# A Mamba block between two RWKV FFNs: in eight of 64 steps GpSimd does the product by C

## The chip, the cores and the metric

The kernel runs on one core of one Trainium2 chip. The metric is the device time of a run in microseconds. TensorE is called PE here, VectorE DVE, ScalarE ACT, GpSimd POOL and SyncE SP, as in the profile.

## What is computed

An input of 4 sequences of 2048 tokens with 512 features goes through an FFN, a selective state space layer (16 states for each of 1024 inner channels), and the same FFN again. All is float32. Cut to what matters:

```python
def _L0_attn_ref(x, ln_w, ln_b, W_in, W_conv, b_conv, W_xproj, W_dt, b_dt, A_log, D_skip, W_out):
    xn = _layernorm(x, ln_w, ln_b)
    xs, z = jnp.split(jnp.einsum('bld,ed->ble', xn, W_in), 2, axis=-1)
    xp = jnp.pad(xs, ((0, 0), (K_CONV - 1, 0), (0, 0)))
    xc = silu(b_conv + sum(xp[:, k:k + L, :] * W_conv[:, k] for k in range(K_CONV)))   # 4 taps
    dbl = jnp.einsum('ble,re->blr', xc, W_xproj)                                       # x projection
    dt_low, B_ssm, C_ssm = dbl[..., :32], dbl[..., 32:48], dbl[..., 48:]
    delta = softplus(jnp.einsum('blr,er->ble', dt_low, W_dt) + b_dt)
    dA = jnp.exp(delta[..., None] * -jnp.exp(A_log))
    dBx = delta[..., None] * B_ssm[:, :, None, :] * xc[..., None]
    # for each t: h = dA_t * h + dBx_t;  y_t = einsum('bdn,bn->bd', h, C_t)
    y = (ys + D_skip * xc) * silu(z)
    return jnp.einsum('ble,de->bld', y, W_out) + x

def _ffn(x):   # x_prev is x one token earlier
    xr, xk = mu_r * x + (1 - mu_r) * x_prev, mu_k * x + (1 - mu_k) * x_prev
    return sigmoid(xr @ W_r.T) * (square(relu(xk @ W_k.T)) @ W_v.T)

x = x + 0.5 * _ffn(_layernorm(x))
x = x + _L0_attn_ref(_layernorm(x), ...)
x = x + 0.5 * _ffn(_layernorm(x))
```

## The kernel before

**Tiling.** The tokens are cut into 16 chunks of W = 512 tokens. The program is a pipeline over iterations: in iteration `it` the scan of chunk `it` runs, beside it the front of chunk `it + 1` (`f`: first FFN, xs, convolution, x projection) and the back of chunk `it - 1` (`b`: output projection, second FFN). The iterations before chunk 0 and behind chunk 15 hold what is left of these. An iteration has 64 steps: step `s` is state `s % 16` of a quarter `s // 16` of the 1024 channels, 256 channels as two tiles of 128 partitions, so that an operation of the scan is 128 x 1024.

**A step.** POOL makes `dbx` = u times B (`product`, L1283; 4 buffers), ACT makes `decay` = exp(delta A) in PSUM (`make_decay`, L877; 2 buffers, three activations), DVE scans in place in `decay` (`scan`, L1078) and multiplies it by C into `g` (`weigh`, L1088; 2 buffers in SBUF), PE adds `g` into `y_acc` by eight transposes (`sum_g`, L556), and ACT keeps the last state (`save`, L892). ACT may make decay `s` once it has saved `s - 2`; POOL's product `s` waits for DVE's product by C of `s - 4`, and DVE's `weigh` of `s` for PE's sum of `s - 2`. B and C rows come from DRAM, a DMA from SP for each.

**Order.** Every engine executes its queue in order. What stands where is written in tables, one number or tuple for a kind of work: the step behind whose scan work it is put. `XS`, `TAP0`/`TAPS`, `ADD_HEAD`, `CTANH` and `CSILU` are the eight tiles of the convolution: PE's matmuls `xs`, ACT's `conv_start` (L792), DVE's three taps (L1031), POOL's `add_head` (L1262) and ACT's `conv_tanh` (L806) and DVE's `conv_silu` (L1034). POOL's `add_head(e)` stands in step `ADD_HEAD[e]`, one to four steps behind the taps, because POOL's queue runs some steps ahead of DVE's. `XPROJ` are the two halves of the x projection (`xproj`, L523), and `XROWS` = 51 is ACT's `x_rows` (L813), which takes it from PSUM. `keep_y` (L860) takes `y_acc` out in steps 17, 33, 49 and 65. `MM_K`, `MM_R`, `MM_V` are the FFNs' matmuls, `MIX_K`, `MIX_R` DVE's mixing before them, `TANH` and `RELU` ACT's. `MEANS` and `RSTD` end and use the statistics of a layer norm (POOL's Newton steps, some 18 small operations). Two PSUM banks, `mm`, go round among all matmuls by the table `BANK`: a group of matmuls waits until the work before it in its bank has been taken out. `ZEROS` says in which steps PE multiplies by a tile of zeros into `y_acc`: one such `add_zeros` is 128x512, two instructions in the profile, and doesn't change the sum.

## Time and profile before

| | us |
|---|---|
| median of 3 runs (lowest, highest) | 4895.8 (4893.4, 4898.2) |
| the profiled execution, device time | 4895.2 |
| its span from the first to the last instruction | 4893.2 |
| DVE busy in the span | 4486.8 |
| PE busy | 4290.6 |
| POOL busy | 3196.2 |
| ACT busy | 2899.1 |

The profile is one execution. Busy time of an engine leaves out waits, register and semaphore instructions. A row of the timeline has the start in us from the span's start, the time taken, the engine, line and operation, out<-in, and in brackets how long the engine had been idle and who released it. On one engine a row often starts a little before the one ahead of it has ended.

### The profile page before, as it was taken

What the parts mean: (1) busy time and instruction counts of PE and PEld (TensorE: products, weight loads), DVE (VectorE), ACT (ScalarE), POOL (GpSimd) and SP (SyncE); (2) the same over time, 40 slices, a digit from 0 to 9 for tenths busy, and PEclk for the clock granted to TensorE, in tenths of its full rate; (3) what the DMA queues carried; (4) which work ended last, traced back from release to release, by engine and by line L of the source; (5) the groups of instructions that cost most, each with busy time, mean ns of one, the idle gap of its engine ahead of it and who ended that gap; (6) DMA issues with size and microseconds to landing.
All of it is one profiled execution on the core that took longest, in us unless ns stands there. A gap on an engine that the chain in (4) does not pass through costs nothing.

```text
span 4893.2 us, 58099 instructions
## 1 busy us (share of the span) xinstructions
PE 4290.6 (88%) x16896; PEld 2377.8 (49%) x16896; DVE 4486.8 (92%) x3650; ACT 2899.1 (59%) x6355; POOL 3196.2 (65%) x3328
## 2 busy tenths in 40 slices
PE   6777999898999989989898899989989898999787
PEld 2444545454554545545454454545545454554443
DVE  2799999999999999999999999999999999999992
ACT  2555656566666666656666665666656666665452
POOL 1566767676675767767576776767767576776770
PEclk8888999999999999999999999999999999999798
DMA  2345555554554545555555554555555555555551
GB/s 82 128 142 181 171 164 184 172 182 163 188 170 154 189 157 188 175 171 188 161 177 161 188 171 151 190 176 179 173 180 178 153 180 159 188 170 152 166 164 62
DMA packets 423053, 810.71 MB, mean 166 GB/s; under 512 B 41264, under 2 KB 41264, under 8 KB 418640
## 3 DMA queue, kind: packets, MB, share of 16 engines
q1 hardware_dynamic: 422736, 807.00, 51.7%
q8 instruction: 136, 2.23, 0.2%
q14 instruction: 181, 1.48, 0.1%
HBM read 772.25 MB, written 34.60 MB: 165 GB/s over the span
## 4 chain that ended last, share of the span: by engine, by line
DVE 39%; PE 29%; issue 16%; ACT 7%; POOL 6%; DMA 2%; DVEq 0%; SPq 0%; POOLq 0%; ACTq 0%
DVE decay L1085 19%; DVE g L1093 10%; PE y_acc L567 6%; PE mm L494 5%; PE mm L483 5%; PE mm L472 4%; POOL dbx L1292 4%; DVE xc L1031 3%; PE mm L531 2%; DMA c_all<-bc_scratch 2%; PE mm L509 2%; PE mm L519 2%; DVE xc L1037 1%; ACT decay L889 1%; POOL xout L1281 1%
## 5 line engine op out<-in xcount | busy, mean ns | idle before, releaser
L1292 POOL TENSOR_TENSOR dbx<-u,b_all 128x1024 f32<-128x1024 f32 x1024 | 2414.2, 2358 | 902.4 <-DVE g L1093 901.6
L1085 DVE TENSOR_TENSOR_SCAN decay<-decay,state,dbx 128x1024 f32<-128x1024 f32 x1024 | 2404.4, 2348 | 179.5 <-ACT decay L889 178.0
L567 PE MATMUL y_acc<-ident,g 128*128 128x128 f32 x8192 | 1121.0, 282 | 380.2 <-DVE g L1093 378.4
L567 PEld LDWEIGHTS y_acc<-ident,g 128*128 128x128 f32 x8192 | 944.0, 144 | 946.8 <-DVE g L1093 721.9
L1093 DVE TENSOR_TENSOR g<-decay,c_all 128x1024 f32<-128x1024 f32 x1024 | 1243.1, 1214 | 9.1 <-issue 0.8
L886 ACT ACTIVATE decay<-delta,neg_a 128x512 f32<-128x512 f32 x1024 | 708.7, 692 | 36.8
L889 ACT ACTIVATE decay<-delta,neg_a 128x511 f32<-128x511 f32 x1024 | 686.9, 671 | 0.0
L895 ACT ACTIVATE state<-decay 128x2 f32<-128x2 f32 x1024 | 166.8, 163 | 511.2 <-DVE g L1093 509.0
L494 PE MATMUL mm<-wbuf_c,col 128*128 128x512 f32 x1024 | 461.0, 594 | 2.1 <-ACT col L758 1.3
L1031 DVE SCALAR_TENSOR_TENSOR xc<-mm,conv_sb,xc 128x509 f32<-128x509 f32 (+2 forms) x384 | 285.0, 742 | 46.6 <-ACT xs_last L804 35.3
L1296 POOL TENSOR_TENSOR dbx<-dbx,carry 128x1 f32<-128x1 f32 x1024 | 274.3, 268 | 80.3
L494 PEld LDWEIGHTS mm<-wbuf_c,col 128*128 128x128 f32 x1024 | 185.2, 190 | 191.9 <-issue 186.4
L802 ACT ACTIVATE xc<-mm,evec,conv_sb 128x512 f32<-128x512 f32 x128 | 99.4, 777 | 255.5 <-PE mm L509 221.3
L762 ACT ACTIVATE rows<-mm 128x512 f32<-128x512 f32 x128 | 76.2, 595 | 294.3 <-PE mm L483 294.3
L472 PE MATMUL mm<-mix_k,wbuf_c 128*128 128x512 f32 x512 | 233.2, 600 | 4.5 <-DVE mix_k L1008 4.4
L509 PE MATMUL mm<-xn_col,wbuf_d 128*128 128x512 f32 x512 | 235.2, 603 | 1.3 <-ACT xn_col L789 1.0
L483 PE MATMUL mm<-wbuf_d,xin 128*128 128x512 f32 x512 | 231.9, 597 | 4.4 <-DVE xin L1013 4.4
L596 PE MATMUL mm<-wbuf_a,gate 128*128 128x512 f32 x512 | 233.2, 599 | 2.2 <-issue 1.4
L472 PE MATMUL mm<-mix_k,wbuf_b 128*128 128x512 f32 x512 | 233.1, 599 | 1.7 <-DVE mix_k L1008 1.7
L509 PE MATMUL mm<-xn_col,wbuf_a 128*128 128x512 f32 x512 | 232.9, 599 | 1.4 <-DVE xc L1031 1.4
L519 PE MATMUL mm<-xn_col,wbuf_b 128*128 128x512 f32 x512 | 231.3, 595 | 0.0
L519 PE MATMUL mm<-xn_col,wbuf_c 128*128 128x512 f32 x512 | 230.7, 593 | 0.0
(100 smaller groups left out, 5098.7 us busy)
## 6 DMA issues: line engine op xcount, KB each, us to landing
b_all<-bc_scratch SPq DMA_DIRECT2D x1024, 256.0 KB, 3.4
c_all<-bc_scratch SPq DMA_DIRECT2D x1024, 256.0 KB, 3.6
wbuf_d<-in_w_r SPq DMA_DIRECT2D x32, 1024.0 KB, 7.2
wbuf_c<-in_w_v SPq DMA_DIRECT2D x32, 1024.0 KB, 7.2
xin<-in_x SPq DMA_DIRECT2D x16, 1024.0 KB, 7.0
wbuf_c<-in_w_k SPq DMA_DIRECT2D x16, 1024.0 KB, 6.6
wbuf_d<-in_w_in SPq DMA_DIRECT2D x16, 1024.0 KB, 5.7
wbuf_a<-in_w_in SPq DMA_DIRECT2D x16, 1024.0 KB, 8.1
```

The lines of the kernel that those rows point to most:

```text
L472: last = pe.matmul(bank(it, f"f{i}k{j}"), wk[:, ct, j * P:(j + 1) * P], mix_k[:, ct, :], start=ct == 0, stop=ct == CT - 1)
L483: last = pe.matmul(bank(it, f"f{i}r{tb}"), mix_r[:, ct, tb * P:(tb + 1) * P], wr[:, ct, :], start=ct == 0, stop=ct == CT - 1)
L494: last = pe.matmul(bank(it, f"f{i}v{tb}"), col[:, ct, tb * P:(tb + 1) * P], wv[:, ct, :], start=ct == 0, stop=ct == CT - 1)
L509: last = pe.matmul(bank(it, f"xs{e}"), win[:, ct, e % 4 * P:(e % 4 + 1) * P], xn_col[:, slot, ct, :], start=ct == 0, stop=ct == CT - 1)
L519: last = pe.matmul(bank(it, f"z{e}"), win[:, ct, e % 4 * P:(e % 4 + 1) * P], xn_col[:, slot, ct, :], start=ct == 0, stop=ct == CT - 1)
L567: last = pe.matmul(y_acc[:, tb, j * P:(j + 1) * P], g[:, s % PAIRS, j, tb * P:(tb + 1) * P], ident[:, :], start=n == 0 and j == 0 and tb % ...
L886: act.activation(d[:, 0, :], delta[:, q % 2, 0, :], ACT.Exp, scale=neg_a[:, e, n:n + 1]).then_inc(decay_done, 1)
L889: act.activation(d[:, 1, 1:W], delta[:, q % 2, 1, 1:W], ACT.Exp, scale=neg_a[:, e + 1, n:n + 1]).then_inc(decay_done, 1)
L1031: dve.scalar_tensor_tensor(out=o, in0=src[:, 0:W - late], scalar=conv_sb[:, e, q:q + 1], in1=o, op0=ALU.mult, op1=ALU.add).then_inc(m_dve. ...
L1085: dve.tensor_tensor_scan(d, d, flat(dbx[:, s % DBX, :, :]), state[:, batch, s, 0:1], ALU.mult, ALU.add).then_inc(scan_done, 1)
L1093: dve.tensor_tensor(g[:, s % PAIRS, :, :], decay[:, s % PAIRS, :, :], c_all[:, s % CRING, :].unsqueeze(1).broadcast_to([P, QT, W]), ALU.mu ...
L1292: pool.tensor_tensor(dbx[:, s % DBX, :, :], u[:, q % 2, :, :], b_all[:, s % BRING, :].unsqueeze(1).broadcast_to([P, QT, W]), ALU.mult).the ...
```

## The change

Eight steps of 64, 13, 29, 31, 35, 39, 41, 44 and 47 (`POOLED`), are treated in another way. All but 13 are steps with convolution taps on DVE. In these the scan writes its result to `g` in SBUF instead of in place in PSUM, so DVE's `scan` waits for PE's sum of `s - 2`, DVE has no `weigh`, and ACT no `save`. POOL, three steps later in its queue (behind its product `s + 3`), copies the last state (128x2) and multiplies `g` in place by C (`pool_weigh`). PE's sum, SP's load of C four steps on and POOL's product four steps on wait for whichever engine multiplies. ACT's decay of `s + 2` waits for the scan alone.

Beside that, entries of the tables move by a step or two, both halves of the x projection from 49, 50 to 47, 48, five zeros are added (20, 26, 37, 49, 52), and for chunk 1 the first layer norm moves: its POOL part to before `u`, its ACT part from step 58 of iteration -1 to behind the first step of iteration 0. The functions `ffn_norm`, `mamba_inner` and `make_res` are written for one tile at a time; where they stand is as before.

```diff
@@ tables @@
-        TURN = ((0, 0, 1, 1), (35, 35, 35, 35))
+        TURN = ((0, 0, 0, 1), (35, 35, 35, 35))
-        MM_R = ((10, 10, 12, 13), (41, 42, 44, 45))
+        MM_R = ((10, 11, 12, 13), (41, 42, 44, 45))
-        XPROJ = (49, 50)
-        ZEROS = {2: 2, 31: 2, 39: 2, 30: 1, 53: 1}
+        XPROJ = (47, 48)
+        ZEROS = {2: 2, 31: 2, 39: 2, 30: 1, 53: 1, 52: 1, 49: 1, 26: 1, 37: 1, 20: 1}
-        RELU = ((7, 8, 9, 10), (49, 50, 53, 53))
-        TANH = ((11, 13, 14, 14), (42, 43, 45, 46))
+        RELU = ((7, 8, 9, 10), (48, 50, 53, 53))
+        TANH = ((11, 14, 14, 14), (42, 43, 45, 46))
-        MIX_R = ((6, 7, 7, 8), (38, 39, 40, 40))
-        CSILU = (33, 34, 40, 42, 43, 45, 48, 48)
+        MIX_R = ((6, 7, 7, 8), (39, 40, 40, 40))
+        CSILU = (32, 34, 40, 42, 43, 45, 48, 48)
-        OUT_ADD = (6, 22, 23, 25)
-        STATS = ((51, 53, 53, 54), (9, 22, 24, 27), (18, 19, 20, 21))
+        OUT_ADD = (6, 21, 23, 25)
+        STATS = ((51, 53, 53, 54), (9, 22, 24, 27), (18, 18, 20, 21))
-        FFN_ADD = ((18, 19, 20, 22), (57, 58, 59, 60))
+        FFN_ADD = ((17, 19, 20, 22), (57, 58, 59, 60))
-        HISTORY = 26
+        HISTORY = 24
+        POOLED = (13, 29, 31, 35, 39, 41, 44, 47)
...
+        def so_far(it, s, pooled):
+            it, s = it + s // NSTEP, s % NSTEP
+            here = sum(q <= s for q in POOLED)
+            return it * len(POOLED) + here if pooled else it * (NSTEP - len(POOLED)) + s + 1 - here
...
+        def multiplied(it, s):
+            return (pool_mult_done if on_pool(s) else mult_done), so_far(it, s, on_pool(s))
...
@@ sum_g on PE (and likewise load_c on SP, product on POOL) @@
-                pe.wait_ge(mult_done, NSTEP * it + s + 1)
+                pe.wait_ge(*multiplied(it, s))
...
@@ make_decay and save on ACT @@
-                if due(count := NSTEP * it + s - PAIRS + 1):
+                if on_pool(s - PAIRS):
+                    if due(count := NSTEP * it + s - PAIRS + 1):
+                        act.wait_ge(scan_done, count)
+                elif due(count := so_far(it, s - PAIRS, False)):
                     act.wait_ge(saved, count)
...
             def save(it, s, batch):
+                if on_pool(s):
+                    return
...
@@ scan and weigh on DVE @@
-                dve.tensor_tensor_scan(d, d, flat(dbx[:, s % DBX, :, :]), state[:, batch, s, 0:1],
+                if on_pool(s) and due(count := NSTEP * it + s - PAIRS + 1):
+                    dve.wait_ge(g_summed, count)
+                o = flat(g[:, s % PAIRS, :, :]) if on_pool(s) else d
+                dve.tensor_tensor_scan(o, d, flat(dbx[:, s % DBX, :, :]), state[:, batch, s, 0:1],
                                        ALU.mult, ALU.add).then_inc(scan_done, 1)
             def weigh(it, s):
+                if on_pool(s):
+                    return
...
@@ POOL @@
+            def pool_weigh(it, s, batch):
+                pool.wait_ge(scan_done, NSTEP * it + s + 1)
+                pool.sem_inc(passed_pool, 1)
+                states = g[:, s % PAIRS, :, :]
+                pool.tensor_copy(state[:, batch, s, :], states[:, :, W - 1]).then_inc(pool_saved, 1)
+                pool.wait_ge(pool_saved, so_far(it, s, True))
+                pool.sem_inc(passed_pool, 1)
+                pool.wait_ge(c_loaded[s % CRING], it * (16 * NSTEP // CRING) + 16 * (s // CRING + 1))
+                pool.tensor_tensor(states, states, c_all[:, s % CRING, :].unsqueeze(1).broadcast_to([P, QT, W]),
+                                   ALU.mult).then_inc(pool_mult_done, 1)
...
                     if scn:
                         product(it, s)
+                        if s > 2 and on_pool(s - 3):
+                            pool_weigh(it, s - 3, bt)
...
                         if s == MAKE_U[0] + 64:
+                            if it == -1:
+                                ffn_rstd(0, 1)
                             make_u(f, 0, (bt + 1) % BATCHES)
-                    if ahead and s == RSTD[0]:
+                    if ahead and it != -1 and s == RSTD[0]:
                         ffn_rstd(0, it + 2)
...
@@ end of a step on ACT @@
-                    if ahead and s == NORM[0]:
-                        ffn_norm(0, it + 2)
+                    if ahead and it != -1:
+                        for n in at(NORM[0], s):
+                            ffn_norm(0, it + 2, n)
+                    if it == s == 0:
+                        for n in range(TB):
+                            ffn_norm(0, 1, n)
```

POOL, around step 32 of an iteration with scan, front and back, from the end of the second FFN's rstd (before L1216, after L1250) on. L1292 and L1296 (after: L1328 and L1332) are `product`, L1264 (after: L1298) is `add_head(0)`. First before, then after:

```order
L1216 TENSOR_SCALAR shift<-shift 128x4
L1292 TENSOR_TENSOR dbx<-u,b_all 128x1024
L1296 TENSOR_TENSOR dbx<-dbx,carry 128x1
L1292 TENSOR_TENSOR dbx<-u,b_all 128x1024
L1296 TENSOR_TENSOR dbx<-dbx,carry 128x1
L1264 TENSOR_TENSOR xc<-xc,head 128x3
L1292 TENSOR_TENSOR dbx<-u,b_all 128x1024
L1296 TENSOR_TENSOR dbx<-dbx,carry 128x1
```

```order
L1250 TENSOR_SCALAR shift<-shift 128x4
L1328 TENSOR_TENSOR dbx<-u,b_all 128x1024
L1332 TENSOR_TENSOR dbx<-dbx,carry 128x1
L1328 TENSOR_TENSOR dbx<-u,b_all 128x1024
L1332 TENSOR_TENSOR dbx<-dbx,carry 128x1
L1340 COPY state<-g 128x2
L1344 TENSOR_TENSOR g<-g,c_all 128x1024
L1298 TENSOR_TENSOR xc<-xc,head 128x3
L1328 TENSOR_TENSOR dbx<-u,b_all 128x1024
L1332 TENSOR_TENSOR dbx<-dbx,carry 128x1
```

The copy of the state and the product by C of step 29 stand between the product of step 32 and `add_head(0)`.

DVE, steps 28 to 31: L1085 (after: L1117) is `scan`, L1093 (L1127) `weigh`, L1042 (L1069) the gate's silu, L1031 (L1058) the taps. First before, then after:

```order
L1085 SCALAR_TENSOR_TENSOR decay<-decay,state,dbx 128x1024
L1042 SCALAR_TENSOR_TENSOR gate<-gate,mm 128x512
L1093 TENSOR_TENSOR g<-decay,c_all 128x1024
L1085 SCALAR_TENSOR_TENSOR decay<-decay,state,dbx 128x1024
L1031 SCALAR_TENSOR_TENSOR xc<-mm,conv_sb,xc 128x509
L1031 SCALAR_TENSOR_TENSOR xc<-mm,conv_sb,xc 128x510
L1031 SCALAR_TENSOR_TENSOR xc<-mm,conv_sb,xc 128x511
L1093 TENSOR_TENSOR g<-decay,c_all 128x1024
L1085 SCALAR_TENSOR_TENSOR decay<-decay,state,dbx 128x1024
L1042 SCALAR_TENSOR_TENSOR gate<-gate,mm 128x512
L1093 TENSOR_TENSOR g<-decay,c_all 128x1024
L1085 SCALAR_TENSOR_TENSOR decay<-decay,state,dbx 128x1024
```

```order
L1117 SCALAR_TENSOR_TENSOR decay<-decay,state,dbx 128x1024
L1069 SCALAR_TENSOR_TENSOR gate<-gate,mm 128x512
L1127 TENSOR_TENSOR g<-decay,c_all 128x1024
L1117 SCALAR_TENSOR_TENSOR g<-decay,state,dbx 128x1024
L1058 SCALAR_TENSOR_TENSOR xc<-mm,conv_sb,xc 128x509
L1058 SCALAR_TENSOR_TENSOR xc<-mm,conv_sb,xc 128x510
L1058 SCALAR_TENSOR_TENSOR xc<-mm,conv_sb,xc 128x511
L1117 SCALAR_TENSOR_TENSOR decay<-decay,state,dbx 128x1024
L1069 SCALAR_TENSOR_TENSOR gate<-gate,mm 128x512
L1127 TENSOR_TENSOR g<-decay,c_all 128x1024
L1117 SCALAR_TENSOR_TENSOR g<-decay,state,dbx 128x1024
```

The scan of steps 29 and 31 writes `g`, and no `weigh` follows the taps.

PE, steps 47 to 53: L567 (after: L583) is `sum_g`, L472 (L488) the matmuls k of the second FFN, L531 (L547) the halves of the x projection, L575 (L591) zeros, L543 (L559) dt. First before, then after:

```order
L472 MATMUL mm<-mix_k,wbuf_b 128x512 x4
L567 MATMUL y_acc<-ident,g 128x128 x16
L531 MATMUL mm<-xc,wx_sb 64x512 x4
L567 MATMUL y_acc<-ident,g 128x128 x8
L472 MATMUL mm<-mix_k,wbuf_b 128x512 x4
L531 MATMUL mm<-xc,wx_sb 64x512 x4
L567 MATMUL y_acc<-ident,g 128x128 x8
L472 MATMUL mm<-mix_k,wbuf_b 128x512 x4
L567 MATMUL y_acc<-ident,g 128x128 x16
L543 MATMUL mm<-xdbl,wdt_sb 128x512 x2
```

```order
L488 MATMUL mm<-mix_k,wbuf_b 128x512 x4
L547 MATMUL mm<-xc,wx_sb 64x512 x4
L583 MATMUL y_acc<-ident,g 128x128 x8
L547 MATMUL mm<-xc,wx_sb 64x512 x4
L583 MATMUL y_acc<-ident,g 128x128 x8
L591 MATMUL y_acc<-ident,zero 128x512
L583 MATMUL y_acc<-ident,g 128x128 x8
L488 MATMUL mm<-mix_k,wbuf_b 128x512 x4
L583 MATMUL y_acc<-ident,g 128x128 x8
L488 MATMUL mm<-mix_k,wbuf_b 128x512 x4
L583 MATMUL y_acc<-ident,g 128x128 x8
L591 MATMUL y_acc<-ident,zero 128x512
```

Before, the halves of the x projection stand on both sides of the third k; now both stand ahead of it, with a zero between, and another zero follows the fourth k.

## Rows read from the trace of the kernel before

**Rows 1.** The page, its first part: busy us, share of the span, instructions.

```profile
PE 4290.6 (88%) x16896; PEld 2377.8 (49%) x16896; DVE 4486.8 (92%) x3650; ACT 2899.1 (59%) x6355; POOL 3196.2 (65%) x3328
```

**Rows 2.** Costliest groups: count, busy us, mean ns of one, idle before, releaser.

```profile
L1292 POOL TENSOR_TENSOR dbx<-u,b_all 128x1024 f32<-128x1024 f32 x1024 | 2414.2, 2358 | 902.4 <-DVE g L1093 901.6
L1085 DVE TENSOR_TENSOR_SCAN decay<-decay,state,dbx 128x1024 f32<-128x1024 f32 x1024 | 2404.4, 2348 | 179.5 <-ACT decay L889 178.0
...
L1093 DVE TENSOR_TENSOR g<-decay,c_all 128x1024 f32<-128x1024 f32 x1024 | 1243.1, 1214 | 9.1 <-issue 0.8
```

**Rows 3.** Windows, chunks 0, 6, 15: length, busy us by engine, PEclk, DMA share, GB/s.

```profile
161.70:447.20 285.50, 214.39 (x860) 128.62 (x858) 268.01 (x202) 163.59 (x364) 193.53 (x191) 0.86 0.50 158
...
1905.40:2197.40 292.00, 264.08 (x1056) 145.94 (x1056) 280.05 (x229) 180.82 (x397) 199.72 (x207) 0.99 0.53 174
4531.50:4787.30 255.80, 201.16 (x844) 124.65 (x844) 243.59 (x168) 138.44 (x320) 172.70 (x148) 0.87 0.49 160
```

**Rows 4.** Windows of chunk 6, PE, PEld, DVE, ACT, POOL: steps 47-51, then 9-19.

```profile
2121.60:2147.10 25.50, 24.19 (x85) 11.39 (x85) 21.32 (x17) 12.96 (x31) 15.76 (x13) 1.00 0.73 240
...
1944.90:1992.10 47.20, 46.95 (x177) 25.53 (x176) 42.36 (x31) 27.89 (x63) 32.35 (x26) 1.00 0.52 163
```

**Rows 5.** Timeline, chunk 6, steps 13 to 15.

```profile
1963.36 3.67 PE L483 MATMUL mm<-wbuf_d,xn_col 128*128 128x512 f32 x8
...
1967.06 0.60 ACT L762 ACTIVATE rows<-mm 128x512 f32<-128x512 f32 x1 [3.85 <-PE mm L483]
...
1970.47 2.36 DVE L1085 TENSOR_TENSOR_SCAN decay<-decay,state,dbx 128x1024 f32<-128x1024 f32 x1 [3.62 <-ACT decay L889]
```

**Rows 6.** Timeline, chunk 6, steps 29 to 32.

```profile
2031.34 2.32 DVE L1031 SCALAR_TENSOR_TENSOR xc<-mm,conv_sb,xc 128x509 f32<-128x509 f32 x3
...
2031.74 2.37 POOL L1292 TENSOR_TENSOR dbx<-u,b_all 128x1024 f32<-128x1024 f32 x1
...
2034.32 0.20 POOL L1264 TENSOR_TENSOR xc<-xc,head 128x3 f32<-128x3 f32 x1
...
2034.55 0.63 ACT L811 ACTIVATE rows<-xc 128x512 f32<-128x512 f32 x1 [1.76 <-POOL xc L1264]
...
2039.21 1.02 PE L575 MATMUL y_acc<-ident,zero 128*128 128x512 f32 x2
...
2045.92 2.36 DVE L1085 TENSOR_TENSOR_SCAN decay<-decay,state,dbx 128x1024 f32<-128x1024 f32 x1 [0.30 <-ACT decay L889]
```

**Rows 7.** Timeline, chunk 6, steps 46 to 53.

```profile
2121.84 3.60 PE L472 MATMUL mm<-mix_k,wbuf_b 128*128 128x512 f32 x8
...
2132.11 1.09 PE L567 MATMUL y_acc<-ident,g 128*128 128x128 f32 x8 [1.31 <-DVE g L1093]
...
2144.85 0.69 ACT L820 ACTIVATE xdbl<-mm,xscale 64x512 f32<-64x512 f32 x1 [7.63 <-PE mm L531]
...
2147.11 2.36 DVE L1085 TENSOR_TENSOR_SCAN decay<-decay,state,dbx 128x1024 f32<-128x1024 f32 x1 [4.05 <-ACT decay L889]
...
2150.78 1.09 PE L567 MATMUL y_acc<-ident,g 128*128 128x128 f32 x8 [0.56 <-DVE g L1093]
```

**Rows 8.** Timeline of DVE and POOL, chunk 0, step 7; last row chunk 6, step 40.

```profile
190.05 2.34 DVE L1085 TENSOR_TENSOR_SCAN decay<-decay,state,dbx 128x1024 f32<-128x1024 f32 x1
192.31 2.76 DVE L1013 SCALAR_TENSOR_TENSOR xn_col<-col,vec,xn_col 128x512 f32<-128x512 f32 x2
...
191.52 2.34 POOL L1292 TENSOR_TENSOR dbx<-u,b_all 128x1024 f32<-128x1024 f32 x1
...
2087.77 1.57 DVE L1013 SCALAR_TENSOR_TENSOR xin<-col,vec,xin 128x512 f32<-128x512 f32 x2
```

**Rows 9.** Timeline of the start, POOL and DVE.

```profile
149.85 2.34 POOL L1270 TENSOR_TENSOR u<-delta,xc 128x1024 f32<-128x1024 f32 x1 [12.37 <-ACT delta L837]
...
161.74 2.36 DVE L1085 TENSOR_TENSOR_SCAN decay<-decay,state,dbx 128x1024 f32<-128x1024 f32 x1 [20.16 <-ACT decay L889]
```

99 lines of the change are left out of this document (54 added, 45 removed).

## The prediction

> **What bounds the kernel now.** I read the busy shares first [rows 1], then the costliest groups [rows 2], then the stretches of the program [rows 3, 4], and last the timeline at the places that the change touches [rows 5 to 9]. The reader is to see that DVE is busy for 92% of the span and PE for 88%, so neither has much to give. Of each step the scan costs 2.35 us and the product by C 1.21 us of DVE [rows 2]; a row begins 0.08 us before the one ahead of it ends (190.05 + 2.34 against 192.31 [rows 8]), so a product takes 1.13 us of the chain. Fourteen of the sixteen chunks are alike; the row of one of them, 292.0 us, stands for all [rows 3]: DVE busy 280.1, so idle 11.9; PE busy 264.1, so idle 27.9. Two of the DVE's waits make up most of its idle time. In step 15 it waits 3.62 us for a decay, which ACT makes only after a tanh whose matmul ends on PE at 1967.03 [rows 5]; PE is busy for 46.95 of 47.20 us there [rows 4]. In step 52 it waits 4.05 us for ACT, which had stood 7.63 us behind the x projection [rows 7].
>
> **What each part costs, if nothing else moves.** Eight products by C leave DVE: 8 x 1.13 = 9.0 us of a chunk. POOL takes on a copy of 128x2, by its other small operations 0.20 us [rows 6], and a product of 128x1024 with one operand broadcast, which is exactly the form of its product dbx<-u,b_all: 2.36 us [rows 2]; together about 2.65 us with the gaps of 0.08, so 21 us a chunk of an engine that is idle for 92 of 292 us. The x projection two steps sooner is to take away the 4.05 us. The five added zeros cost PE 0.87 to 0.93 us each (a zero is two instructions, 1.02 us [rows 6], less the overlap), 4.6 us a chunk. The scan that writes SBUF is not in the trace. Its bound comes from the DVE's other operations on PSUM and SBUF: the taps write SBUF, and their three take 2.32 us while POOL's product runs all the time beside them [rows 6]. I take 2.35 us, and 0.05 us either way for the range: 128 scans, 6 us. DMAs are not touched, except that a load of C is issued after POOL's product in a pooled step; it is four steps ahead of its use. The naive sum is (9.0 + 4.05) x 16 = 209 us. Most of it isn't to be had, for the reasons that follow.
>
> **Step 13: nothing.** The wait of step 15 hangs on PE's matmuls, which stand back to back from step 5 on. DVE arrives 1.13 us sooner and waits 4.75 instead of 3.62 us. POOL's product of step 13 begins after its product of step 16, near 1962.8, and ends near 1965.4, before PE has ended the matmul at 1967.03, behind which it asks for it [rows 5]. The zero of step 20 comes behind that stretch.
>
> **Steps 29 to 32: a loss of 2.8 us.** In POOL's queue the new product stands behind two products for dbx and ahead of add_head(0) [the order of POOL]. POOL is late here already: it had rstd work and works without a break until add_head(0) at 2034.32, and ACT waits 1.76 us for that before tanh(0), decay(31) and the gate [rows 6]. One DVE operation put into step 21 (an out_add, 0.6 us) delays the means, and all this queue, by another 0.6. So: dbx products of steps 31 and 32 end at 2034.9, copy and product for step 29 at 2037.55, add_head(0) at 2037.7, tanh(0) 2038.35, decay(31) 2039.7, gate tanh 2040.2. DVE, which stands at the gate in step 30, goes on 3 us later than it did. The tap of step 31 and ACT's four normalisations follow PE's xs; the scan of step 32 starts at 2048.7 instead of 2045.92 [rows 6]. Both pooled products before it have gained nothing.
>
> **Steps 33 to 47.** The same walk goes on with the durations of the trace. Step 35 gives 1.13 back, the zero in 37 and POOL's late product of 35 take it again (PE's transposes wait for it, then ACT, then the taps): scan 38 is 2.6 us late. In 38 to 41 DVE finds its old slack and two pooled steps: scan 42 is 0.5 us late. Then a collision counts. A DVE operation with two inputs in SBUF (mix_k, mix_r, silu) that starts while POOL's product runs ends only 0.55 us after it: two such take 1.57 us where POOL is about to end and 2.76 us where it has just begun [rows 8]. Before the change POOL starts its product right behind the DVE's, so it ends as the scan ends, and a collision costs 0.2 us. After a pooled step POOL goes straight on to its next dbx product, 5.7 us after the last product of DVE, and DVE's next two-input operation comes at 6.7 us. That happens in steps 42, 45 and 48, for some 1.1 us each: 3.3 us of the gain of the three. Scan 47 starts 1.3 us late and PE's first ffn_k matmul at 2123.3 instead of 2121.84 [rows 7].
>
> **Steps 48 to 63.** Now k1 and both halves of the x projection run on PE until 2139.1 (it was 2144.8), ACT isn't held by x_rows any more, and scan 52 comes at 2145.8 instead of 2147.11: the wait of 4.05 us is gone, but 1.2 us of the DVE's come back at keep_y of step 49, which waits for transposes that stand behind the first half of the projection. What is late next is PE. It was busy for 24.2 of the 25.5 us of steps 47 to 51 [rows 4] and had 1.31 + 0.56 us to spare until step 53 [rows 7]; the zeros of 49 and 52 take 1.8 us. So the matmuls of step 54 start 0.7 us later than they did, and from there to step 61 PE has no gap, and DVE follows it. The end of a chunk is then between 0 and 0.5 us late. I take 0 for each of the fourteen, with 2.2 us sooner (no collisions, POOL not late by the 0.6) and 2 us later as its bounds.
>
> **Start and ends.** In iteration -1 the rstd of chunk 1 now comes before u, when POOL waits 12.37 us anyway [rows 9], and ACT's four normalisations of that chunk come after the first decay. The first dbx product then starts at 152.4, right behind u, instead of behind the rstd, and the first scan at 155.1 instead of 161.74 [rows 9]: 6.6 us, once. Chunk 0 (285.5 us, DVE idle 17.5) and chunk 15 (255.8, idle 12.2) have only one of the FFNs beside the scan and PE at 75 to 79% [rows 3], so a part of their 9.0 us is real: I take 7 and 5 us, between 0 and 12 together as bounds below and 18 above.
>
> **Sum.** Against the profiled execution (4895.2 us, span 4893.2, median of the runs 4895.8): 14 x 0 + 6.6 + 7 + 5 = 18.6 us less, 4877 us.
>
> **A page of the notes.** The row of the collision is [rows 8]: 2.76 us for two operations that take 1.57 elsewhere. The Trainium skill, page "SBUF — State Buffer", section "Who interferes with whom", says that a VectorE instruction with two SBUF inputs and a GpSimd instruction that reads SBUF contend for one port pair, and that the second to issue fully blocks. By that rule, the trace agrees, the three collisions stand. If they cost only the usual 0.2 us, the chunk would end 2.2 us sooner, 4846 us. The same section says that an instruction with at most one SBUF input doesn't contend, which would leave the new scan alone; no row shows that scan.
>
> **Rivals.** (B) POOL isn't late where I have it late and the collisions stay small: each chunk ends 2.2 us sooner, 4877 - 31 = 4846 us; for it speaks POOL's idle third, against it [rows 6, 8]. (C) DVE was the bound all through, and the gains of 29 to 47 and the projection mostly arrive: 5.5 us a chunk, 4800 us; against it speaks PE's share in steps 47 to 61. (D) Slower: POOL's lateness is carried on. If its dbx product behind a pooled step is still late when the next one is due, the two-input operations of steps 34, 43 and 46 collide in full too, each for up to 1.2 us; 3.6 us less the slack of 1.6 is 2 us a chunk, 4877 + 28 = 4905 us. It decides once POOL is more than 0.9 us behind after the second product. (E) The change does nothing at all in the chunks but for the start: 4889 us; it lies within the forecast's own range.
>
> **How the numbers follow.** Forecast 0.45 (4865 to 4892), B 0.25, C 0.08, D 0.22. Within 0.2%, 9.8 us, a measurement of this kernel can hardly tell a difference. Faster than 4886: 0.34 of the forecast, B and C, 0.67; the same: 0.11 of the forecast and 0.07 of D, 0.18; slower 0.15. The range from 4825 to 4904 leaves out C and the far half of D, and holds the unknown of the scan.
>
> **What would show it.** In the changed profile: DVE's wait for ACT in step 52 gone; in step 30 a DVE wait of 3 us at the gate, and ACT's wait for add_head grown to 4 to 5 us; mix_k and silu in steps 42, 45 and 48 with 1.9 us in place of 0.9; DVE's wait in step 15 at 4.7 us; PE's gap of 0.56 us at step 52 gone; the first scan at 155 us. I am wrong if the scan into SBUF isn't 2.35 us, if POOL's product by C isn't 2.36 us, or if a typical chunk is not 290 to 294 us long.

## The result and the profile after

The changed kernel takes 4909.8 us (median of 10 runs, 4907.9 to 4913.1) against 4895.9 us (4892.2 to 4898.2) before: a ratio of 1.0029, 95% interval 1.0020 to 1.0037. It is slower by 0.3%, where 4877 us and a range up to 4904 had been predicted. The profiled execution spans 4907.1 us (4893.2 before).

The profile page of the changed kernel, its first part, against [rows 1]:

```profile
PE 4351.3 (89%) x17056; PEld 2423.2 (49%) x17056; DVE 4385.7 (89%) x3522; ACT 2882.0 (59%) x6227; POOL 3497.3 (71%) x3584
```

DVE has lost 101 us of work, POOL has gained 301, PE 61. The engine that was the busiest was relieved, and the kernel got longer. The costliest groups, against [rows 2]; L1344 is POOL's product by C, L1117 the scan in its two forms:

```profile
L1328 POOL TENSOR_TENSOR dbx<-u,b_all 128x1024 f32<-128x1024 f32 x1024 | 2414.8, 2358 | 746.2 <-DVE g L1127 738.2
L1117 DVE TENSOR_TENSOR_SCAN decay<-decay,state,dbx 128x1024 f32<-128x1024 f32 x896 | 2105.2, 2350 | 188.6 <-ACT decay L908 169.9
...
L1127 DVE TENSOR_TENSOR g<-decay,c_all 128x1024 f32<-128x1024 f32 x896 | 1089.0, 1215 | 15.9 <-PE y_acc L583 6.8
...
L1344 POOL TENSOR_TENSOR g<-g,c_all 128x1024 f32<-128x1024 f32 x128 | 301.6, 2356 | 24.0 <-POOL state L1340 22.9
L1117 DVE TENSOR_TENSOR_SCAN g<-decay,state,dbx 128x1024 f32<-128x1024 f32 x128 | 299.5, 2339 | 4.9 <-ACT decay L908 4.6
```

The windows of chunks 0, 6 and 15 (length; busy us of PE, PEld, DVE, ACT, POOL; granted clock, DMA share, GB/s), against [rows 3]:

```profile
153.00:434.20 281.20, 221.69 (x874) 133.24 (x874) 261.33 (x194) 163.54 (x359) 214.57 (x207) 0.86 0.51 164
1900.40:2193.60 293.20, 267.86 (x1066) 149.22 (x1066) 273.65 (x221) 179.86 (x389) 218.47 (x223) 0.99 0.53 173
4538.60:4799.10 260.50, 208.43 (x854) 127.60 (x854) 237.94 (x160) 136.79 (x312) 191.22 (x164) 0.87 0.48 157
```

DVE's idle time is 19.6 us in chunk 6 (11.9 before) and 22.6 in chunk 15 (12.2 before). The 13.9 us of the two spans divide as follows: the first scan comes 8.8 us sooner; chunk 0 is 4.2 us shorter; chunks 1 to 14 are 20.1 us longer together; chunk 15 is 4.7 us longer, and what follows its last scan 2.1 us.

To see where in a chunk that happens, I took the start of each scan from the timeline, counted from the chunk's first scan, as the mean of chunks 2 to 14, and subtracted the same of before:

| scan | 30 | 31 | 32 | 38 | 42 | 47 | 50 | 52 | 55 | 64 |
|---|---|---|---|---|---|---|---|---|---|---|
| changed, us late | -1.3 | 3.0 | 4.2 | 3.5 | 1.1 | 2.0 | 3.7 | -0.5 | 1.3 | 1.3 |
| predicted | | | 2.8 | 2.6 | 0.5 | 1.3 | | -1.3 | | 0 |

The first difference from the prediction arises by scan 32. First a row of the kernel before, whose xs of step 30 no row above shows, then the timeline of the changed kernel there, chunk 6 (start, us, engine and line; in brackets the idle time before and who ended it), against [rows 6]:

```profile
2035.77 3.60 PE L509 MATMUL mm<-xn_col,wbuf_d 128*128 128x512 f32 x8
```

```profile
2030.22 2.34 POOL L1344 TENSOR_TENSOR g<-g,c_all 128x1024 f32<-128x1024 f32 x1 [0.18 <-POOL state L1340]
2032.52 0.19 POOL L1298 TENSOR_TENSOR xc<-xc,head 128x3 f32<-128x3 f32 x1
...
2032.62 1.22 PE L583 MATMUL y_acc<-ident,g 128*128 128x128 f32 x8 [3.10 <-POOL g L1344]
2033.63 5.20 PE L525 MATMUL mm<-xn_col,wbuf_d 128*128 128x512 f32 x8
...
2032.74 0.63 ACT L827 ACTIVATE rows<-xc 128x512 f32<-128x512 f32 x1 [5.12 <-POOL xc L1298]
...
2038.87 0.78 ACT L818 ACTIVATE xc<-mm,evec,conv_sb 128x512 f32<-128x512 f32 x1 [3.70 <-PE mm L525]
...
2035.21 0.69 DVE L1069 SCALAR_TENSOR_TENSOR gate<-gate,mm 128x512 f32<-128x512 f32 x1 [4.46 <-ACT gate L891]
...
2045.40 2.36 DVE L1117 TENSOR_TENSOR_SCAN decay<-decay,state,dbx 128x1024 f32<-128x1024 f32 x1 [1.44 <-ACT decay L908]
```

Two chains start at POOL's product of step 29. One runs by add_head(0), which stands behind it on POOL, to ACT's tanh, decay(31) and the gate that DVE waits for. The other runs over PE, which has the sum of that g ahead of the eight matmuls of xs: it waits 3.10 us, and xs then takes 5.20 us where the same matmuls took 3.60 before. The windows of the wait, of the sum, and of xs (columns as above; the last three are clock, DMA share and GB/s):

```profile
2029.50:2032.60 3.10, 0.01 (x1) 0.00 (x0) 1.25 (x1) 0.00 (x0) 2.84 (x5) 1.00 0.55 172
2032.60:2033.80 1.20, 1.18 (x9) 1.19 (x10) 0.00 (x0) 1.05 (x2) 1.18 (x2) 0.85 0.14 51
2033.80:2038.80 5.00, 5.00 (x10) 2.07 (x9) 3.59 (x3) 1.37 (x4) 3.08 (x3) 0.69 0.36 124
```

After standing idle for 3.1 us, PE works for a while at the lower of its two levels, 1.2 GHz: a mean of 0.69 over the 5 us of xs. That differs from chunk to chunk: in chunks 2 to 14 xs of that step takes 3.6 to 5.3 us, 4.6 in the mean (3.6 in all of before). In chunks 3 and 9, where it takes 3.6, scan 32 is 2.8 and 2.9 us late; in the other eleven it is 4.2 to 4.8 us late. The Trainium skill, page "TensorE: Matmul & The Clock Gate", section "Part 1: The HAM clock gate", says that the array's clock goes back to half rate when the engine has been idle; the trace agrees here, with 0.69 behind the wait of 3.10 us.

The trace of the kernel before already had such places, at the start of a chunk, where I had not looked. In each of chunks 1 to 14 PE waits 2.55 to 2.88 us ahead of the sum in step 0, and in eight of the fourteen it then works at half clock: the transposes behind take up to 1.92 us, in the other six 1.04. Timeline and window of before, chunk 6, then the same place in chunk 5:

```profile
1905.56 1.33 PE L567 MATMUL y_acc<-ident,g 128*128 128x128 f32 x8 [2.55 <-DVE g L1093]
1906.69 1.92 PE L458 MATMUL mm<-ident,rows 128*128 128x128 f32 x8
...
1905.50:1909.90 4.40, 3.85 (x21) 3.45 (x22) 4.37 (x4) 4.28 (x10) 3.25 (x3) 0.61 1.02 276
...
1613.84 1.09 PE L567 MATMUL y_acc<-ident,g 128*128 128x128 f32 x8 [2.55 <-DVE g L1093]
1614.77 1.04 PE L458 MATMUL mm<-ident,rows 128*128 128x128 f32 x8
```

### The profile page after: what moved, and what is told of

The parts are those of the page before. It is cut to its first block, busy times and chain, and to the rows that moved or that the text cites. A ratio compares the mean times of both kernels' runs of the same rounds, so it can differ in the third digit from the quotient of the medians.

```text
span 4907.1 us, 58559 instructions
## 1 busy us (share of the span) xinstructions
PE 4351.3 (89%) x17056; PEld 2423.2 (49%) x17056; DVE 4385.7 (89%) x3522; ACT 2882.0 (59%) x6227; POOL 3497.3 (71%) x3584
## 4 chain that ended last, share of the span: by engine, by line
PE 38%; DVE 20%; POOL 17%; issue 14%; ACT 8%; DMA 3%; SPq 0%; DVEq 0%; POOLq 0%; ACTq 0%
POOL dbx L1328 10%; PE y_acc L583 8%; DVE decay L1117 7%; PE mm L488 7%; PE mm L499 7%; PE mm L510 5%; DVE g L1127 4%; PE mm L525 4%; DMA c_all<-bc_scratch 2%; PE mm L547 2%; DVE xc L1058 2%; PE mm L535 2%; DVE g L1117 1%; POOL g L1344 1%; PE mm L559 1%
## 5 line engine op out<-in xcount | busy, mean ns | idle before, releaser
L1328 POOL TENSOR_TENSOR dbx<-u,b_all 128x1024 f32<-128x1024 f32 x1024 | 2414.8, 2358 | 746.2 <-DVE g L1127 738.2
L1117 DVE TENSOR_TENSOR_SCAN decay<-decay,state,dbx 128x1024 f32<-128x1024 f32 x896 | 2105.2, 2350 | 188.6 <-ACT decay L908 169.9
L583 PE MATMUL y_acc<-ident,g 128*128 128x128 f32 x8192 | 1118.7, 282 | 358.1 <-DVE g L1127 269.8
L583 PEld LDWEIGHTS y_acc<-ident,g 128*128 128x128 f32 x8192 | 960.3, 144 | 915.8 <-DVE g L1127 495.8
L1127 DVE TENSOR_TENSOR g<-decay,c_all 128x1024 f32<-128x1024 f32 x896 | 1089.0, 1215 | 15.9 <-PE y_acc L583 6.8
L916 ACT ACTIVATE state<-decay 128x2 f32<-128x2 f32 x896 | 147.0, 164 | 569.4 <-DVE g L1127 567.4
L1058 DVE SCALAR_TENSOR_TENSOR xc<-mm,conv_sb,xc 128x509 f32<-128x509 f32 (+2 forms) x384 | 285.5, 743 | 54.4 <-ACT xs_last L820 43.4
L1332 POOL TENSOR_TENSOR dbx<-dbx,carry 128x1 f32<-128x1 f32 x1024 | 263.4, 257 | 80.3
L1344 POOL TENSOR_TENSOR g<-g,c_all 128x1024 f32<-128x1024 f32 x128 | 301.6, 2356 | 24.0 <-POOL state L1340 22.9
L1117 DVE TENSOR_TENSOR_SCAN g<-decay,state,dbx 128x1024 f32<-128x1024 f32 x128 | 299.5, 2339 | 4.9 <-ACT decay L908 4.6
L525 PE MATMUL mm<-xn_col,wbuf_d 128*128 128x512 f32 x512 | 248.9, 632 | 1.3 <-ACT xn_col L805 1.0
L499 PE MATMUL mm<-wbuf_d,xin 128*128 128x512 f32 x512 | 243.2, 621 | 4.4 <-DVE xin L1040 4.4
L488 PE MATMUL mm<-mix_k,wbuf_c 128*128 128x512 f32 x512 | 232.6, 598 | 4.5 <-DVE mix_k L1035 4.4
```

Source lines behind the costliest of these rows:

```text
L488: last = pe.matmul(bank(it, f"f{i}k{j}"), wk[:, ct, j * P:(j + 1) * P], mix_k[:, ct, :], start=ct == 0, stop=ct == CT - 1)
L499: last = pe.matmul(bank(it, f"f{i}r{tb}"), mix_r[:, ct, tb * P:(tb + 1) * P], wr[:, ct, :], start=ct == 0, stop=ct == CT - 1)
L525: last = pe.matmul(bank(it, f"xs{e}"), win[:, ct, e % 4 * P:(e % 4 + 1) * P], xn_col[:, slot, ct, :], start=ct == 0, stop=ct == CT - 1)
L583: last = pe.matmul(y_acc[:, tb, j * P:(j + 1) * P], g[:, s % PAIRS, j, tb * P:(tb + 1) * P], ident[:, :], start=n == 0 and j == 0 and tb % ...
L1058: dve.scalar_tensor_tensor(out=o, in0=src[:, 0:W - late], scalar=conv_sb[:, e, q:q + 1], in1=o, op0=ALU.mult, op1=ALU.add).then_inc(m_dve. ...
L1117: dve.tensor_tensor_scan(o, d, flat(dbx[:, s % DBX, :, :]), state[:, batch, s, 0:1], ALU.mult, ALU.add).then_inc(scan_done, 1)
```

## Experiments in steps 29 to 33

Typical chunk means the mean of chunks 2 to 14, as its difference from before (negative is shorter). All ratios are to the kernel before as it was timed beside each run; its medians were 4895.9 to 4898.2 us, so a difference of two runs in us carries some 2 us of that. The chunk differences come from one profiled execution each.

**e1_no_29_31** and **e8_no_29.** In e1 both products go back to DVE, in e8 only that of step 29:

```diff
-        POOLED = (13, 29, 31, 35, 39, 41, 44, 47)
+        POOLED = (13, 35, 39, 41, 44, 47)       # e1
+        POOLED = (13, 31, 35, 39, 41, 44, 47)   # e8
```

> The changed kernel, with the products by C of steps 29 and 31 given back to DVE; six pooled steps stay. Theory T (the loss is made in steps 29 to 33: the changed trace has scan 33 of a chunk 4.8 us later than before, because POOL is already late there, PE waits 3.1 us for POOL's product of step 29 and then runs its next eight matmuls at the half clock, 5.2 us for 3.6): scan 33 within 0.5 us of where it was before the change, scan 47 1 to 2.5 us sooner than before, a typical chunk 289 to 290.5 us for 293.2, 4850 to 4880 us. Rival C (collisions on DVE and the added zeros make the loss, and 29 and 31 give their 1.13 us each like the others): a typical chunk 294 to 295.5 us, 4925 to 4945 us.

> The changed kernel with only the product by C of step 29 back on DVE; 31 stays on POOL. Theory T (the loss of 3.9 us a chunk hangs on the product of 29, which stands ahead of add_head(0) and makes PE wait 3.1 us ahead of xs): step 30 back to 4.3 to 5 us, no matmul of xs at the half clock, scan 33 within 1 us of the place without both, 289 to 290.5 us a chunk, 4848 to 4870 us. Rival B (each of the two makes half of the loss): 291 to 291.5 us a chunk, 4876 to 4886 us.

Measured: e1 4848.9 us (0.9903, 0.9889 to 0.9916), chunk -2.6; e8 4845.0 us (0.9891, 0.9878 to 0.9905), chunk -2.8. Scan 33 is 0.8 and 0.5 us late in place of 4.8, and xs of step 30 takes 3.60 us in every chunk of both. The product of step 29 alone costs 65 us of the kernel. With it gone, that of step 31 seems worth 4 us; the intervals of e1 and e8 overlap, but e12 less e7, below, differ by the same step and by 6.5 us. Rival B is out, and rival C in what it says of 29 and 31; that the zeros and the collisions cost time too is shown below.

**e9_filled.** PE's order and waits stay; the idle time is filled:

```diff
                     elif scn:
+                        if s == 30:
+                            add_zeros(3)
                         sum_g(it, s - 1)
```

> The changed kernel with three zeros (six matmuls of nothing, 2.7 us) in step 30 ahead of PE's sum of the g of step 29, where PE stands idle for 3.1 us; nothing else is moved. Theory K (the idle time itself is not what the eight matmuls of xs pay for, it is the half clock that follows it): the granted clock stays at 1.00, xs takes 3.6 us in place of 5.2, scan 32 comes 1.3 to 1.6 us sooner, and the chunk ends between 0 and 1.5 us sooner, 4885 to 4910 us. Rival (xs is slow for another reason, its weights or a port): xs 5.2 us as it was, 4907 to 4915 us.

Measured: 4888.6 us (0.9985, 0.9976 to 0.9994), chunk -0.1. Windows of e9 over the filled wait, the sum and xs, then xs in its timeline:

```profile
2023.70:2026.90 3.20, 2.74 (x7) 0.95 (x5) 1.40 (x1) 0.00 (x0) 2.94 (x5) 1.00 0.52 173
2026.90:2028.10 1.20, 1.11 (x9) 1.11 (x10) 0.00 (x0) 0.98 (x2) 1.18 (x3) 1.00 0.21 61
2028.10:2033.10 5.00, 5.00 (x19) 2.56 (x19) 3.52 (x3) 2.99 (x8) 3.08 (x3) 1.00 0.48 118
```

```profile
2027.92 3.60 PE L525 MATMUL mm<-xn_col,wbuf_d 128*128 128x512 f32 x8
```

The clock stays at 1.00 and xs is back at 3.60 us. Six matmuls of nothing make the kernel 21 us faster, since PE had nothing else to do there. Scan 32 is 2.8 us late and the chunk ends 0.1 us early: these are the 2.8 and 0 of the prediction. So the half clock is the term it lacked in steps 29 to 32. That the end comes out too is partly luck: scans 38, 42 and 47 of e9 are 2.1 us late, 0.3 us early and 0.6 us late where 2.6, 0.5 and 1.3 late were foretold, and steps 48 to 63 make up 0.7 us where 1.3 were foretold.

**e5_sum_behind, e10_head_first, e11_both.** Each of the two chains is freed alone, and then both:

```diff
+        BEHIND = (29,)                              # e5, e11
...
-                    elif scn:                       # PE, top of a step (e5, e11)
+                    elif scn and s - 1 not in BEHIND:
                         sum_g(it, s - 1)
...
+                    if scn and s - 1 in BEHIND:     # PE, end of a step, ahead of the zeros
+                        sum_g(it, s - 1)
...
-                        if s > 2 and on_pool(s - 3):    # POOL (e10, e11)
+                        if s > 2 and on_pool(s - 3) and s != 32:
                             pool_weigh(it, s - 3, bt)
...
+                    if scn and s == 32:             # POOL, behind add_head
+                        pool_weigh(it, 29, bt)
```

> The changed kernel; only PE's order is changed: it adds the g of step 29 behind the eight matmuls of xs of step 30 and not ahead of them. POOL's queue is as it was, so it is just as late. Theory T (PE's wait for POOL's product and the half clock behind it are most of the loss of steps 31 and 32): xs runs in 3.6 us at the full clock and ends 5 to 6 us sooner, scan 31 stays where it is, scan 32 comes 2 to 3.3 us sooner, a typical chunk 290.5 to 292 us, 4868 to 4892 us. Rival P (POOL's lateness alone, by add_head, the tanh and the decay behind it, sets these steps): scan 33 where it is, 293 us a chunk, 4904 to 4912 us.

> The changed kernel with POOL's copy and product of step 29 behind add_head(0) in step 32 and not ahead of it; PE's order as changed. Theory T (two paths run from that product: by add_head, tanh(0), decay(31) and the gate to DVE in step 30, and by PE's sum, xs and ACT's four normalisations to decay(32); each alone holds scan 32): the DVE's wait for the gate in step 30 falls from 4.5 to about 1.5 us and scan 31 comes 2.5 to 3 us sooner, scan 32 stays within 0.5 us, 4902 to 4914 us. Rival A (the path by add_head alone makes the loss): scan 33 comes 2.5 to 3 us sooner too, 4862 to 4880 us.

> Both at once: POOL's product of step 29 behind add_head(0), and PE's sum of that g behind xs of step 30. The eight pooled steps stay, no work is added or left out. Theory T (with both paths free the product of 29 costs what it costs elsewhere, nothing): scan 33 within 1 us of where it is with 29 on DVE, 289 to 291 us a chunk, 4845 to 4878 us. Rival G (what is won by scan 32 is given back again by step 38, as it was when PE's sum alone stood behind xs): 292.5 to 293.5 us a chunk, 4893 to 4908 us.

Measured: e5 4900.7 us (1.0009, 1.0000 to 1.0018), chunk +1.2; e10 4914.5 us (1.0035, 1.0022 to 1.0049), chunk +1.9; e11 4847.1 us (0.9898, 0.9885 to 0.9912), chunk -2.8. Neither chain alone gives anything in the profiled chunks; both together give all that taking the step out gives. The profiled executions of e5 and e10 lie 4 and 5 us above their medians, so their chunks are shown a little too long. By the medians freeing PE alone is worth 9 us of the 65, freeing POOL's chain alone nothing. In e10, DVE's wait at the gate of step 30 falls from 4.46 to 1.82 us, and 4.05 us appear at gate_y in step 31, behind the same PE (timeline of e10):

```profile
2036.47 0.69 DVE L1069 SCALAR_TENSOR_TENSOR gate<-gate,mm 128x512 f32<-128x512 f32 x1 [1.82 <-ACT gate L891]
...
2045.10 0.69 DVE L1075 TENSOR_TENSOR gate<-gate,mm 128x512 f32<-128x512 f32 x1 [4.05 <-PE mm L601]
```

In e5 my expectation was wrong. Scan 32 did come 2.9 us sooner, but all but 0.1 of it was gone by scan 38. Timeline of PE in e5:

```profile
2027.52 3.60 PE L526 MATMUL mm<-xn_col,wbuf_d 128*128 128x512 f32 x8
...
2035.35 1.36 PE L584 MATMUL y_acc<-ident,g 128*128 128x128 f32 x8 [2.50 <-DVE g L1130]
...
2039.32 3.62 PE L592 MATMUL y_acc<-ident,zero 128*128 128x512 f32 x4
```

Its windows of steps 31 and 35 to 36:

```profile
2035.20:2040.40 5.20, 4.17 (x18) 3.29 (x19) 5.08 (x6) 4.46 (x9) 4.67 (x4) 0.58 0.41 124
...
2055.20:2064.20 9.00, 7.09 (x43) 6.22 (x41) 7.98 (x6) 6.20 (x15) 7.80 (x8) 0.81 0.29 95
```

PE had done xs sooner, and stood idle behind it for DVE, which was late by the other chain. The half clock came there (0.58, zeros of 1.88 us in 3.62) and again at 2055 (0.81), where the changed kernel has 1.00. Most of the idle time had only moved. That the second stretch takes the last of the gain back is read from the trace; no run shows it by itself.

## Experiments on the collisions and the zeros

**e2_no_41_44_47.** `POOLED = (13, 29, 31, 35, 39)`.

> The changed kernel, with the products by C of steps 41, 44 and 47 given back to DVE. Theory T (each of the three saves 1.13 us and the two-input DVE operation one step later, beside POOL's next product, takes 1.0 of it back): steps 42, 45 and 48 go back to 4.8 to 4.9 us from 5.8 to 5.9, and a typical chunk is 293.0 to 293.8 us for 293.2, 4903 to 4918 us. Rival (the three are a real gain that something else eats up later): 295 to 296.5 us a chunk, 4935 to 4955 us.

Measured: 4922.4 us (1.0054, 1.0042 to 1.0067), chunk +2.0, 0.8 more than the changed kernel. Expected were 4903 to 4918 us; the three are worth a little more than I had thought, 0.8 us a chunk together, 12.6 us in all, where DVE gives up 3 x 1.13 us of each. What takes it back (timeline of the changed kernel, steps 42, 45, 48 of chunk 6, against [rows 8]):

```profile
2096.00 1.90 DVE L1035 SCALAR_TENSOR_TENSOR mix_k<-col,vec,mix_k 128x512 f32<-128x512 f32 x1
...
2111.10 2.00 DVE L1035 SCALAR_TENSOR_TENSOR mix_k<-col,vec,mix_k 128x512 f32<-128x512 f32 x1
...
2125.70 2.52 DVE L1064 SCALAR_TENSOR_TENSOR xc<-rows,xc 128x512 f32<-128x512 f32 x2
...
2094.99 2.36 POOL L1328 TENSOR_TENSOR dbx<-u,b_all 128x1024 f32<-128x1024 f32 x1
```

mix_k of step 42 ends at 2097.90, 0.55 us after POOL's product (2097.35). It takes 0.91 us in step 43. The Trainium skill, page "SBUF — State Buffer", section "Who interferes with whom", has a VectorE instruction with two SBUF inputs blocked by a GpSimd instruction that reads SBUF and was issued first; the trace agrees, with 1.90 us for 0.91. It also says that a VectorE instruction with at most one SBUF input, outside its 2-port modes, doesn't contend, and the scan into SBUF agrees with that: 2.34 us in the mean of all 128, of which 125 ran beside a product of POOL for more than half of their time.

**e3_no_zeros** takes `52: 1, 49: 1` out of ZEROS; **e6_no_29_31_zeros** does so in e1.

> The changed kernel without the zeros of steps 49 and 52 (two matmuls each). Theory T (PE has no gap from step 47 to 61 and sets the pace there): both zeros count in full, 0.86 us each, so steps 49 and 54 become 0.8 us shorter each, 291.4 to 291.9 us a chunk, 4882 to 4892 us. Rival C (DVE or ACT holds those steps; PE's zeros lie beside): 293 us a chunk, 4904 to 4912 us.

> The changed kernel, 29 and 31 back on DVE, and without the zeros of steps 49 and 52. Theory T (PE has no gap from 47 to 61 and sets the pace there, whenever it begins): the 1.7 us of both zeros add to the 3.9 us of the two steps, 287.2 to 287.6 us a chunk, 4816 to 4832 us. Rival (with DVE no longer late by 4 us the end of the chunk is DVE's or ACT's, and the zeros lie beside): 289 us a chunk, 4843 to 4851 us.

Measured: e3 4877.6 us (0.9963, 0.9950 to 0.9975), e6 4824.2 us (0.9849, 0.9836 to 0.9863); chunks -1.0 and -4.3. Expected were 4882 to 4892 us for e3, so it gained more than I thought; e6 lies in its range. The two zeros cost 32 and 25 us: 1.7 us a chunk, and they fall due at scan 55, not 0.8 us in each of two steps as I had written. In e3 another 0.7 us is gone by scan 32: xs of step 30 takes 4.0 us in its mean for 4.6, and is slow in four of chunks 2 to 14 for eleven. Why the clock falls less often there, no run tells. The changed kernel at that place: PE's busy time in steps 47 to 53 and 54 to 60, and then PE's zero of step 52, ACT's wait in step 49 and DVE's two waits:

```profile
2119.00:2150.20 31.20, 31.20 (x114) 15.37 (x114) 29.25 (x22) 18.15 (x41) 20.77 (x17) 1.00 0.69 236
2150.20:2181.10 30.90, 30.90 (x121) 17.29 (x120) 28.32 (x27) 19.95 (x41) 24.26 (x33) 1.00 0.32 105
```

```profile
2146.74 1.02 PE L591 MATMUL y_acc<-ident,zero 128*128 128x512 f32 x2
...
2131.98 1.09 ACT L884 ACTIVATE y_rows<-y_acc 128x512 f32<-128x512 f32 x2 [5.35 <-PE y_acc L583]
...
2134.66 2.36 DVE L1117 TENSOR_TENSOR_SCAN decay<-decay,state,dbx 128x1024 f32<-128x1024 f32 x1 [1.35 <-ACT decay L908]
...
2156.28 2.36 DVE L1117 TENSOR_TENSOR_SCAN decay<-decay,state,dbx 128x1024 f32<-128x1024 f32 x1 [1.99 <-ACT decay L908]
```

The trace shows not one gap of PE in 62 us at full clock. Here a zero buys no clock and costs its whole 0.86 us. The same instruction gains in step 30 (e9) and loses in steps 49 and 52.

**e7_moved** is e6 with the two-input operations moved out of the steps behind 41 and 44:

```diff
-MIX_K = (..., (42, 43, 45, 46))              CSILU = (32, 34, 40, 42, 43, 45, 48, 48)
+MIX_K = (..., (43, 43, 46, 46))              CSILU = (32, 34, 40, 43, 43, 46, 48, 48)
```

> As the run before it (29 and 31 on DVE, no zeros in 49 and 52), and the DVE operations with two SBUF inputs of steps 42 and 45 one step later, in 43 and 46, where POOL's product by C of the pooled step is done: mix_k in 43, 43, 46, 46 for 42, 43, 45, 46, and silu(3) and silu(5) in 43 and 46. The work is the same. Theory T (the collision with POOL's late dbx product costs 1.0 us in each of the two): steps 42 + 43 and 45 + 46 become 1.0 us shorter each, scan 47 comes 1.8 to 2.1 us sooner and PE passes it on, 285.2 to 285.9 us a chunk, 4786 to 4804 us. Rival (the collision only moves, or the wait for mix_k and for the tanh takes its place): within 6 us of the run before it.

Measured: 4804.6 us (0.9809, 0.9796 to 0.9823), chunk -5.7, 1.3 less than e6. Scan 47 comes 1.5 us sooner than in e6, where 1.8 to 2.1 were expected, and the time is 0.6 us above the expected range. Timeline of e7, steps 43 and 46:

```profile
2058.77 2.36 DVE L1117 TENSOR_TENSOR_SCAN decay<-decay,state,dbx 128x1024 f32<-128x1024 f32 x1 [0.81 <-ACT decay L908]
2061.03 1.39 DVE L1035 SCALAR_TENSOR_TENSOR mix_k<-col,vec,mix_k 128x512 f32<-128x512 f32 x2
...
2074.93 1.72 DVE L1035 SCALAR_TENSOR_TENSOR mix_k<-col,vec,mix_k 128x512 f32<-128x512 f32 x2
```

The collisions are gone (0.70 and 0.86 us each for 1.90 and 2.00); 0.81 us come back as a wait for ACT's decay of step 43.

## Each part alone, and what paid together

**e4_none_pooled**: `POOLED = ()`, all else as changed.

> The changed kernel with every product by C on DVE, so no scan writes SBUF; the x projection, the zeros and all the rest stay as changed. With six pooled steps (13, 35, 39, 41, 44, 47) it took 4848.9 us, and scan 49 of a chunk came 2.1 us sooner than before the change. Theory T (those five behind step 33 are worth 2.0 us of a chunk by step 49, and from 47 on PE passes that on): 290.8 to 291.7 us a chunk for 289.1, 4872 to 4890 us. Rival X (the gain of the run without 29 and 31 is all the x projection's, the pooled steps give nothing): 4845 to 4855 us.

Measured: 4876.4 us (0.9955, 0.9942 to 0.9969), chunk -1.0, as theory T has it. Against it the seven steps without 29 (e8) are worth 31 us; the eight cost 33.

The next three put one part of the change into the kernel before.

**e13_start_only** takes the conditions `it != -1`, ffn_rstd(0, 1) ahead of make_u, and the four normalisations behind the first decay, with the tables of before. **e14_pooled_only** takes POOLED and its functions, again with the tables and the start of before. **e15_xproj_only**:

```diff
-        XPROJ = (49, 50)                 RELU = (..., (49, 50, 53, 53))
+        XPROJ = (47, 48)                 RELU = (..., (48, 50, 53, 53))
```

> The kernel before with the start of the changed one and nothing else: rstd of chunk 1 ahead of u in iteration -1, its four normalisations behind the first decay. Theory T (the start is a gain of its own, of which chunk 0 gives 1.8 us back in its first four steps, where DVE had no need of what came late before): first scan at 152.5 to 154.5 us for 161.7, chunk 0 1.4 to 1.8 us longer, 4887 to 4892 us. Rival (chunk 0, in which PE and DMA are waited for, gives all of it back): 4893 to 4898 us.

> The kernel before with the eight pooled steps and nothing else: order, zeros, x projection and start as before the change. Theory T (the loss of steps 29 to 33 belongs to the product of 29, not to the moved tables, and the x projection at its old place passes a late scan 48 on): scan 33 of a chunk 3.5 to 4.8 us later than before, scan 47 1 to 2 us, 292.5 to 294 us a chunk for 291.7, 4908 to 4930 us. Rival S (the DVE's old wait of 4.05 us in step 52 takes it up): 291.7 us a chunk, 4890 to 4900 us. Rival M (without the moved out_add of step 21 POOL is 0.6 us less late and the eight steps gain what DVE saves): under 4880 us.

> The kernel before with both halves of the x projection two steps sooner (and with the relu of step 49 in 48, without which PE and ACT would wait for each other) and nothing else. Theory T (its worth is the 4.2 us of step 51 less the 1.8 us that keep_y then waits in step 49; the run without pooled steps has it together with two zeros that cost 1.7 us): 2.2 to 2.8 us a chunk, 4856 to 4868 us. Rival (PE's order alone gives 1 us, the rest of that run's gain was the other moved tables'): 4876 to 4886 us.

Measured: e13 4892.1 us (0.9989, 0.9980 to 0.9998); e14 4922.4 us (1.0054, 1.0040 to 1.0067), scan 33 3.6 us late, chunk +1.8; e15 4863.8 us (0.9931, 0.9919 to 0.9943), chunk -2.2. From the 4896.4 us that the three share: start -4.3, pooled steps +26.0, x projection -32.7, and +32.2 for the zeros of 49 and 52 (changed less e3). The sum is +21; the whole change measures +13.9, so the other moves and the parts' effect on each other are worth some -7 us. That rest is not a measured thing: of the 32.2 us some 0.7 us a chunk is the clock of step 30 (above), and with the 24.7 us that the zeros cost where step 29 is on DVE (e1 less e6) the sum is +13.7, and nothing is left for the rest.

At the start of the changed kernel (timeline, against [rows 9]) the first scan comes 8.8 us sooner, but the product behind it waits for a DMA that nobody had needed so early:

```profile
152.95 2.36 DVE L1117 TENSOR_TENSOR_SCAN decay<-decay,state,dbx 128x1024 f32<-128x1024 f32 x1 [13.34 <-POOL dbx L1332]
156.71 1.23 DVE L1127 TENSOR_TENSOR g<-decay,c_all 128x1024 f32<-128x1024 f32 x1 [1.41 <-DMA c_all<-bc_scratch]
```

By scan 4, 7.0 us are left (6.6 in e13). Chunk 0 of e13 is 2.9 us longer than before, where 1.4 to 1.8 were expected.

**e12_best** is e7 with 31 pooled too; **e16_all_eight** has all eight steps with e11's two orders, no zeros in 49 and 52, and e7's moves.

> All that paid put together: the changed kernel with the product of step 29 on DVE (31 stays on POOL), without the zeros of 49 and 52, and with mix_k in 43, 43, 46, 46 and silu(3) and silu(5) in 43 and 46. From the runs: the same with 31 on DVE too took 4804.6 us, and 31 on POOL was worth 3.9 us beside the product of 29 on DVE. Theory T: they add, 4797 to 4806 us. Rival: the place of 31 matters only because of what the zeros left, 4803 to 4812 us.

> The changed kernel with all eight pooled steps and every cause mended: POOL's product of 29 behind add_head(0), PE's sum of it behind xs of step 30, no zeros in 49 and 52, mix_k in 43, 43, 46, 46 and silu(3) and silu(5) in 43 and 46. Against the fastest kernel so far (4798.0 us) it differs by step 29 alone. Theory T (a product by C in a step where it makes nobody wait is worth nothing by itself, since steps 30 to 33 hang on PE and ACT): within 5 us of 4798. Rival (DVE's 1.13 us of that step arrive now): 4775 to 4788 us.

Measured: e12 4798.0 us (0.9795, 0.9782 to 0.9808), chunk -6.2; e16 4803.0 us (0.9808, 0.9795 to 0.9822), chunk -5.9. e12 is 2.0% faster than before and the fastest here; its profiled execution lies 5 us under the median, so its chunk is shown a little too short. Its DVE is busy for 4373.8 us, 12 less than in the changed kernel, which is 112 us longer: the difference is waiting. Step 29's own 1.13 us of DVE are worth nothing even when they harm nobody (e16).

## Why the prediction was wrong

**Durations: right.** The scan into SBUF takes 2.34 us and POOL's product by C 2.36; 2.35 and 2.36 were assumed.

**Step 13: right.** Step 13 is 1.26 us shorter, and all but 0.2 us of that goes into the wait ahead of the scan of step 15, 4.70 us where 4.75 were foretold (timeline of the changed kernel, against [rows 5]):

```profile
1965.22 2.36 DVE L1117 TENSOR_TENSOR_SCAN decay<-decay,state,dbx 128x1024 f32<-128x1024 f32 x1 [4.70 <-ACT decay L908]
```

**"Steps 29 to 32: a loss of 2.8 us": the step that failed.** POOL's part was exact: its product of step 29 ends 132.16 us into chunk 6, and the working put it at 132.12. The loss by scan 32 is 4.2 us. The working let xs follow with its 3.60 us and left out that PE had stood idle ahead of it: the half clock adds 1.60 us there (1.4 by scan 32 in the mean of the chunks, changed less e9). e9, which removes that and nothing else, gives 2.8 us at scan 32, 0 at the chunk's end and 4888.6 us in all. This term is 21 of the 33 us by which I missed. It was put at nothing without a look at what PE had done after its other waits, and the rows of before at 1905.56 show the half clock behind a wait of 2.55 us.

**Steps 33 to 47: right in kind, too pessimistic by 0.7 us.** From scan 32 to scan 47 the kernel makes up 2.2 us, where 1.5 were foretold, both in the changed kernel and in e9. So of the 1.4 us too much at scan 32 only 0.65 are left at scan 47. The three collisions cost 1.0 us each (1.1 foretold).

**Steps 48 to 63: right in kind, short by 0.6 us.** The chunk's end is 1.3 us late, half of it from before scan 48. The wait of 4.05 us is gone and 1.8 us come back at keep_y (1.2 foretold). PE is what is late next, without a gap. But PE began late and had nothing to make that up with, so a late scan 47 is passed on in full: changed less e9, it is 1.4 us at scan 47 and 1.4 us at the end. My bound of 0.5 us for the chunk's end rested on the 2.8 us above. In e9 this error and that of steps 33 to 47 cancel.

**"Chunk 0 ... and chunk 15 ...: I take 7 and 5 us": wrong.** Chunk 0 gave 4.2 us and chunk 15 lost 4.7. I argued from PE's share of 75 to 79% that DVE is the bound there. Chunk 15 is shorter than before by more than 0.2 us in only two runs (252.7 us in e1, 251.8 in e6, for 253.5), from first to last scan. PE's idle time there has the price of step 30 (timeline of the changed kernel, step 41 of chunk 15):

```profile
4707.02 1.97 PE L583 MATMUL y_acc<-ident,g 128*128 128x128 f32 x8 [3.11 <-DVE g L1127]
4708.78 5.65 PE L499 MATMUL mm<-wbuf_d,xin 128*128 128x512 f32 x8
```

e8 takes 4.4 of the 4.7 us away and e9 2.2, which speaks for step 29 again; but e3, which keeps step 29 on POOL, takes 3.5 away. How the 4.7 us divide stays open.

**Start:** 8.8 us for 6.6, less the 1.8 that chunk 0 gives back. The first scan comes at 152.1 to 154.9 us in the fifteen profiled kernels with the new start, so part of the difference is scatter. **The end,** from the start of the last scan on, takes 108.3 to 109.1 us in ten of the 18 kernels profiled here and 109.7 to 110.4 in the other eight, in no order that I can connect with their edits; its 2.1 us stay open. In the spans the miss of 32.5 us adds up as 20.1 us in chunks 1 to 14, 2.8 in chunk 0, 9.7 in chunk 15 and 2.1 at the end, less 2.2 at the start.

**Rivals.** D gave 4905 us, close to the measurement, by a mechanism that did not occur: steps 34, 43 and 46 last 4.22, 4.83 and 4.22 us as they did before, so POOL's lateness was not carried into them. What did occur, a clock that falls because PE waits, was none of the cases, and the range ended where D ended.

**The signs.** DVE's wait at the gate of step 30 is 4.46 us and not 3: scan 31 is 3.0 us late as foretold, but DVE also arrives 1.3 us sooner. The three signs of being wrong did not show: 2.34 us, 2.36 us, and a typical chunk of 293.0 us in the band of 290 to 294. That band was too wide to tell: 2 us a chunk are 28 us of the kernel, as much as separates the forecast from rival D.

## What to carry to other kernels

When work moves from a full engine to one with idle time, ask who stands behind it in three queues: the receiving engine's, that of the engine that consumes the result in order, and the one behind that. Here one such product of eight turned a gain of 31 us into a loss of 33. When the consumer is TensorE, count its wait twice, once as the wait and once as the matmuls that may run at the lower clock behind it (1.4 us in the mean here), and look in the old trace for what its other waits did; a late operand that is put behind other matmuls helps little (9 of 65 us) while something else makes it idle. Filler on TensorE pays where it would stand idle and costs its full time where it has no gap, so look at the gaps of the very steps.

## What the runs showed of the hardware

After 3.10 us of idle time, the next eight 128x512 matmuls took 5.20 us for 3.60, with a granted clock of 0.69; with all but 0.55 us of that idle time filled, the clock stayed at 1.00. The length of the wait alone does not tell it: in e5 the clock was low from a wait of 2.50 us to the zeros 4 us later; in e10 xs took 4.53 us after 3.27 us of waiting; in the changed kernel itself two of 13 chunks show no slow xs; and in the kernel before, a wait of 2.55 to 2.88 us had the half clock behind it in eight chunks of 14. A scan that reads its decays from PSUM and writes SBUF is no slower than one that writes PSUM (2.339 and 2.350 us).
